# Edge tables of a graph-network kernel loaded for four turns at once, with a table of their own for the scatter pass

## What is computed

```python
# layer 0, twice; layer 3 the same with 8 heads of 16 features
xj = (x @ Wl + bl)[src]
e = leaky_relu(xj + (x @ Wr + br)[dst], 0.2)
logits = e @ att
ex = exp(logits - segment_max(logits, dst)[dst])
out = segment_sum(ex / segment_sum(ex, dst)[dst] * xj, dst)
# layer 2: the score is a sum of two numbers per edge, its message a gathered row
score = leaky_relu(logit[dst] + logit_src[src] + b1)
# layer 1: the edge's two ends are exchanged: its sums go to the unsorted side
agg = segment_sum(exp(leaky_relu(p1[src] + p2[dst])) * emb[dst], src)
```

## Time and profile before

| | us |
|---|---|
| median of 3 runs | 14,991.36 |
| lowest, highest | 14,955.31, 14,998.18 |
| the profiled execution, its time | 14,998.32 |
| its span, first to last instruction | 14,996.4 |
| POOL busy in the span | 9,489.8 (63%) |
| PE busy | 11,026.0 (74%) |
| DVE busy | 7,973.5 (53%) |
| ACT busy | 5,541.4 (37%) |

### The profile page before, as it was taken

How to read it: one execution, slowest core, us unless ns; L and a number is a source line. 1 busy time by engine, 2 the same in 40 slices (tenths; PEclk the granted TensorE clock), 3 DMA queues, 4 the chain that set the end, 5 groups by cost and what they waited for, 6 DMA issues and landing times.

```text
span 14996.4 us, 278163 instructions
## 1 busy us (share of the span) xinstructions
PE 11026.0 (74%) x60653; PEld 8678.6 (58%) x60653; DVE 7973.5 (53%) x29240; ACT 5541.4 (37%) x14105; POOL 9489.8 (63%) x8593
## 2 busy tenths in 40 slices
PE   5777777777777778888888875555555767777776
PEld 4666666666666666666666653344344556666664
DVE  6555555555555555555555553333333566666666
ACT  1444444344444444333333343333333622222223
POOL 3666666466666657888888865566666255655555
PEclk7887788788778775766666765555555877888777
DMA  3111111221111113444444452222222221222222
GB/s 87 45 45 44 44 45 45 88 80 44 45 44 45 44 40 44 39 39 39 39 39 39 39 104 58 44 45 45 45 45 45 60 52 48 50 49 49 50 50 56
DMA packets 808955, 748.01 MB, mean 50 GB/s; under 512 B 264685, under 2 KB 691174, under 8 KB 808254
## 3 DMA queue, kind: packets, MB, share of 16 engines
q0 software_dynamic: 453440, 550.05, 21.1%
q1 hardware_dynamic: 354814, 191.38, 4.9%
HBM read 548.62 MB, written 192.13 MB: 49 GB/s over the span
## 4 chain that ended last, share of the span: by engine, by line
PE 27%; another core or an unknown queue 15%; issue 13%; DMA 9%; DVE 7%; ACT 6%; POOL 2%; SPq 1%; DVEq 1%; ACTq 0%; POOLq 0%
DMA scatter_s<-dst_side 8%; PE bank L738 8%; PE bank L721 3%; PE bank L722 3%; PE bank L1214 3%; ACT oh_e L826 2%; PE bank L1220 2%; PE bank L1229 2%; PE bank L747 2%; PE bank L705 1%; POOL scatter_s L1181 1%; DVE agg L960 1%; DVE lrelu L915 1%; DVE agg L951 1%
## 5 line engine op out<-in xcount | busy, mean ns | idle before, releaser
L738 PE MATMUL bank<-rows,oh_e 128*128 128x130 f32 x9984 | 2172.6, 376 | 1578.7 <-ACT oh_e L826 1172.1
L1181 POOL DMA_INDIRECT scatter_s<-dst_side x1664 | 2568.6, 1544 | 551.9 <-DMA scatter_s<-dst_side 267.1
L738 PEld LDWEIGHTS bank<-rows,oh_e 128*128 128x128 f32 x9984 | 1804.0, 264 | 1918.7 <-issue 1036.4
L826 ACT ACTIVATE oh_e<-bank,weight,minus_w 128x128 f32<-128x128 f32 x4992 | 1880.3, 459 | 2378.4 <-remote 1620.8
L951 DVE SCALAR_TENSOR_TENSOR agg<-agg,rescale,bank 128x130 f32 x4992 | 1683.4, 337 | 1636.6 <-remote 792.6
L722 PE MATMUL bank<-rows,ident 128*128 128x128 f32 x9984 | 2335.9, 319 | 144.8 <-issue 141.1
L687 POOL DMA_INDIRECT rows<-gather_c,edge_sb x1664 | 1650.9, 992 | 1122.4 <-issue 443.9
L687 POOL DMA_INDIRECT rows<-gather_b,edge_sb x1664 | 1672.5, 1005 | 1061.9 <-issue 423.0
L687 POOL DMA_INDIRECT rows<-gather_a,edge_sb x1664 | 1669.1, 1003 | 1008.5 <-issue 412.0
L687 POOL DMA_INDIRECT rows<-gather_s,edge_sb x1664 | 1574.3, 946 | 1061.2 <-issue 443.2
L722 PEld LDWEIGHTS bank<-rows,ident 128*128 128x128 f32 x9984 | 1894.7, 235 | 159.7 <-issue 157.6
(11 more groups left out here) (352 smaller groups left out, 18169.2 us busy)
## 6 DMA issues: line engine op xcount, KB each, us to landing
rows<-gather_a,edge_sb POOLq DMA_INDIRECT x1664
rows<-gather_b,edge_sb POOLq DMA_INDIRECT x1664
scatter_s<-dst_side POOLq DMA_INDIRECT x1664
rows<-gather_s,edge_sb POOLq DMA_INDIRECT x1664
rows<-gather_c,edge_sb POOLq DMA_INDIRECT x1664
rows<-scatter_s SPq DMA_DIRECT2D x56, 455.0 KB, 6.3
scatter_s<-zeros SPq DMA_DIRECT2D x64, 390.0 KB
edge_sb<-edge_tab SPq DMA_DIRECT2D x520, 40.0 KB
```

The costliest lines, as they stand in the source:

```text
L738: ins = e.matmul(sum_bank(g)[:, (g % 2) * AW:(g % 2) * AW + L.aw], oh_e[:, g % 8, :], r, start=True, stop=True)
L826: e.activation(oh_e[:, g % 8, :], bank[7][:, (g % CH) * P:(g % CH + 1) * P], ACT.Relu, bias=weight[:, it.slot(2, 2), g:g + 1], scale=minus ...
L1181: e.indirect_dma_start(scatter_s[k], bass.IndirectOffsetOnAxis(ap=S_.target[:, it.slot(1), g:g + 1], axis=0), S_.summed[:, g % 8, :], None ...
```

## The change

`edge_tab` keeps only the two parts that the gather passes read, and a row of it holds four groups: 128 numbers (512 bytes) per partition. `edge_sb` has eight places of 32 columns, two sets of four turns. SyncE loads a set at every fourth turn, on semaphores of its own (`edge_tables_in`, two of them), ahead of that turn's other tables; `tables_in_slot` counts one DMA less. GpSimd waits for the set's semaphore at every fourth turn and no longer for `tables_in_slot`. The loops of SyncE and GpSimd have bodies of eight turns.

The scatter pass gets its own table `edge_tab_s` of 48 columns per group. It loads one group per turn as before, into the same memory (`S_.edges`).

In the preparation `edge_tab` is stored in 13 pieces, one per 8 groups, each issued in the next tile's round; `edge_tab_s` is stored in one DMA after all of them and after the last store of `gather_a`. E0's opening no longer waits for it. Only the clearing of `agg` does, since the staging area lies in `agg`; `E0.clearing` says so. `tables_saved` counts the 13 pieces and the two row tables.

```diff
+def quad_of(it):
+    return Turn(it.n // QUAD, it.j, it.per // QUAD)
...
-    ET = 5 * G
-    edge_tab = dram("edge_tab", (NG, P, ET))
+    assert NG % (2 * QUAD) == 0
+    ET, ES = 2 * G, 3 * G
+    edge_tab = dram("edge_tab", (NG // QUAD, P, QUAD * ET))
+    edge_tab_s = dram("edge_tab_s", (NG, P, ES))
...
-        edge_sb = sb("edge_sb", [P, U, ET])
+        edge_sb = sb("edge_sb", [P, 2 * QUAD, ET])
...
+            def edges_of(c):
+                w.wait_ge(edges_made.at(c))
+                lo, hi = c * GC // QUAD, (c + 1) * GC // QUAD
+                e.dma_start(edge_tab[lo:hi, :, :].rearrange("q p k -> p q k"),
+                            edge_stage[:, c * GC:(c + 1) * GC, :].rearrange("p (q g) k -> p q (g k)", g=QUAD)).then_inc(tables_saved, 16)
...
+                if c:
+                    edges_of(c - 1)
                 sp_dense0(e, D, "D", c)
-            w.wait_ge(edges_made.at(SC - 1))
-            e.dma_start(edge_tab.rearrange("g p k -> p g k"), edge_stage).then_inc(edge_saved, 16)
             for t in range(SC, NBT):
                 sp_dense0(e, D, "D", t)
+            e.dma_start(edge_tab_s.rearrange("g p k -> p g k"), edge_stage_s).then_inc(edge_saved, 16)
...
-            es = edge_stage[:, c * GC:(c + 1) * GC, :]
-            part = lambda n: es[:, :, n * G:(n + 1) * G]
+            part = lambda stage, n: stage[:, c * GC:(c + 1) * GC, n * G:(n + 1) * G]
             ps = lambda n: bank[c % 2][:, n * P:(n + 1) * P].rearrange("p (g k) -> p g k", k=G)
             mt = mtmp.rearrange("p (g k) -> p g k", k=G)
             w.wait_ge(tile_turned.at(c))
-            own.did(e.tensor_copy(part(0).bitcast(I32), ps(1)))
-            own.did(e.tensor_copy(part(1), ps(0)))
-            own.did(e.tensor_scalar(part(2), ps(0), 0.0, NEG, ALU.is_lt, ALU.mult))
+            own.did(e.tensor_copy(part(edge_stage, 0).bitcast(I32), ps(1)))
+            own.did(e.tensor_scalar(part(edge_stage, 1), ps(0), 0.0, NEG, ALU.is_lt, ALU.mult))
             own.did(e.tensor_scalar(mt, ps(0), P - 0.5, NEG, ALU.is_gt, ALU.mult))
-            own.did(e.tensor_copy(part(3), ps(1)))
-            own.did(e.tensor_copy(part(4), ps(2)))
-            w.wait_ge(own.so_far())
-            e.tensor_tensor(part(2), part(2), mt, ALU.add).then_inc(edges_made.sem, 1)
+            own.did(e.tensor_copy(part(edge_stage_s, 1), ps(1)))
+            own.did(e.tensor_copy(part(edge_stage_s, 2), ps(2)))
+            w.wait_ge(own.so_far())
+            own.did(e.tensor_tensor(part(edge_stage_s, 0), part(edge_stage, 1), mt, ALU.add))
+            w.wait_ge(own.so_far())
+            e.tensor_copy(part(edge_stage, 1), part(edge_stage_s, 0)).then_inc(edges_made.sem, 1)
...
-                self.tab = counts.landing("tables_in_slot", U, 3 + heads, NG)
+                self.tab = counts.landing("tables_in_slot", U, 2 + heads, NG)
+                self.edges_in = counts.landing("edge_tables_in", 2, 1, NG // QUAD)
...
-                e.dma_start(edge_sb[:, u, :], edge_tab[bass.ds(i, 1), :, :].rearrange("o p k -> (o p) k")).then_inc(L.tab.sem(it), 16)
+                if it.n % QUAD == 0:
+                    q, k = quad_of(it), it.slot(0, 2 * QUAD)
+                    w.hold_ge(L.edges_in.at(q, lag=2))
+                    e.dma_start(edge_sb[:, k:k + QUAD, :].rearrange("p t k -> p (t k)"),
+                                edge_tab[bass.ds(q.number(), 1), :, :].rearrange("o p k -> (o p) k")).then_inc(L.edges_in.sem(q), 16)
                 e.dma_start(oh_rows[0:3, u, :], onehot_tab[:, bass.ds(i * (G * P), G * P)]).then_inc(L.tab.sem(it), 16)
...
-            turns(e, NG, 0, turn)
+            long_turns(e, NG, 0, turn, 2 * QUAD)
...
-                u = it.slot()
-                w.hold_ge(L.tab.at(it))
+                u, k = it.slot(), it.slot(0, 2 * QUAD)
+                if it.n % QUAD == 0:
+                    w.hold_ge(L.edges_in.at(quad_of(it)))
...
-                                             bass.IndirectOffsetOnAxis(ap=edge_sb[:, u, g:g + 1].bitcast(I32), axis=0)
+                                             bass.IndirectOffsetOnAxis(ap=edge_sb[:, k, g:g + 1].bitcast(I32), axis=0)
...
+            for point in L.clearing:
+                w.wait_ge(point)
             e.memset(agg[:, :, :], 0.0).then_inc(L.cleared.sem, 1)
...
-                                    view(edge_sb[:, u, 2 * G:], [(0, heads), (1, G)]), ALU.add).then_inc(L.masked.sem, 1)
+                                    view(edge_sb[:, it.slot(0, 2 * QUAD), G:], [(0, heads), (1, G)]), ALU.add).then_inc(L.masked.sem, 1)
...
+        E0.clearing = [(edge_saved, 16)]
```

More of the change, by code:

```diff
@@ L22 @@
 LEAD = 10
+QUAD = 4
 AW = 136
@@ L317, in build @@
         row_made = counts.events("group_rows_made", 1, 1)
-        row_saved = counts.sem("group_rows_saved")
+        tables_saved = counts.sem("group_tables_saved")
         ones_in_rows = counts.sem("ones_in_onehot_rows")
@@ L329, in build @@
         kcol = big2[:, 2 * S:2 * S + SC * P]
-        edge_stage = big1[:, 0:NG * ET].rearrange("p (g k) -> p g k", k=ET)
-        spare = lambda lo, n: big1[:, NG * ET + lo:NG * ET + lo + n]
+        edge_stage_s = big1[:, 0:NG * ES].rearrange("p (g k) -> p g k", k=ES)
+        spare = lambda lo, n: big1[:, NG * ES + lo:NG * ES + lo + n]
         mtmp = spare(0, P)
@@ L336, in build @@
         row8 = spare(3 * P, R8)[0:NG, :]
+        edge_stage = spare(4 * P + R8, NG * ET).rearrange("p (g k) -> p g k", k=ET)
         def tile_set(k):
@@ L371, in sp_prep @@
                     w.wait_ge(row_made.at(0))
-                    e.dma_start(row_tab1, row1).then_inc(row_saved, 16)
-                    e.dma_start(row_tab8, row8).then_inc(row_saved, 16)
+                    e.dma_start(row_tab1, row1).then_inc(tables_saved, 16)
+                    e.dma_start(row_tab8, row8).then_inc(tables_saved, 16)
                 if c == COLS_AT + 1:
@@ L393, in sp_prep @@
                 w.wait_ge(source_saved.at(c))
-            e.wait_ge(edge_saved, 16)
-            e.wait_ge(row_saved, 16 * 2)
+            e.wait_ge(tables_saved, 16 * (2 + SC))
             e.wait_ge(ones_in_rows, 1)
@@ L639, in __init__ @@
                 self.masked = one("masked")
-                self.zeroing, self.zeroed = [], None
+                self.zeroing, self.zeroed, self.clearing = [], None, []
             def w_last(self, it, lag, c):
@@ L1114, in __init__ @@
                 self.free, self.saved, self.n = free, saved, 0
+                self.edges = flat3(edge_sb)[:, 0:U * ES].rearrange("p (u k) -> p u k", k=ES)
                 self.src_rows = self.part(U * G * P // 2).bitcast(BF16).rearrange("p (u n) -> p u n", u=U)
@@ L1290, in turn @@
                             e.tensor_scalar(S_.same[:, g % 8, :], bank[2][:, (g % CH) * P:(g % CH + 1) * P],
-                                            edge_sb[:, v, 3 * G + g:3 * G + g + 1], weight[:, it.slot(1, 2), g:g + 1],
+                                            S_.edges[:, v, G + g:G + g + 1], weight[:, it.slot(1, 2), g:g + 1],
                                             ALU.is_equal, ALU.mult).then_inc(S_.same_made.sem, 1)
@@ L1318, in turn @@
                     w.wait_ge(S_.leaky.at(it))
-                    e.tensor_tensor(logit[:, 0:G], logit[:, 0:G], edge_sb[:, u, 2 * G:3 * G], ALU.add).then_inc(S_.masked.sem, 1)
+                    e.tensor_tensor(logit[:, 0:G], logit[:, 0:G], S_.edges[:, u, 0:G], ALU.add).then_inc(S_.masked.sem, 1)
                     w.wait_ge(S_.count.at(it, G - 1))
@@ L1322, in turn @@
                     w.wait_ge(S_.aim.at(it, lag=1))
-                    e.tensor_scalar(S_.target_f, edge_sb[:, u, 3 * G:4 * G], dump_row[:, 0:1], -1.0, ALU.subtract, ALU.mult
+                    e.tensor_scalar(S_.target_f, S_.edges[:, u, G:2 * G], dump_row[:, 0:1], -1.0, ALU.subtract, ALU.mult
                                     ).then_inc(S_.less.sem, 1)
@@ L1328, in turn @@
                     w.wait_ge(S_.moved.at(it))
-                    e.tensor_tensor(S_.target_f, S_.target_f, edge_sb[:, u, 3 * G:4 * G], ALU.add).then_inc(S_.aim_f.sem, 1)
+                    e.tensor_tensor(S_.target_f, S_.target_f, S_.edges[:, u, G:2 * G], ALU.add).then_inc(S_.aim_f.sem, 1)
                     w.wait_ge(S_.aim_f.at(it))
```

9 lines of the change are left out of this document (5 added, 4 removed).

## The result

The changed kernel takes 15,008.9 us (median of 20 runs), the kernel before 14,976.0 (20 runs). The ratio is 1.0023, with a 95% interval of 1.0016 to 1.0030: 34 us slower by the ratio (the medians differ by 33), where 48 us faster was forecast. That is inside the 0.3% that I had called the same, but the interval leaves no doubt of the direction, and it is the other one.

What follows compares the result with a forecast made beforehand. No engine was full; GpSimd's gather turns, waiting mostly for TensorE's side sums, were taken to set the pace. Terms -44 - 5 + 1 = -48 us gave 14,945 us, range 14,820 to 15,050.

Steps and rivals of the forecast that it cites:

- Longer bodies: SyncE's and GpSimd's loops of eight turns instead of four: between 0 and -0.5 us a turn, taken as 0.
- GpSimd's wait: Gather passes: GpSimd waits for one load every fourth turn, so TensorE's waits for rows go: -44 us, bounds 0 and 149.
- SyncE's instructions: Gather loops: fewer edge loads for SyncE to issue with register addresses: -5 us, from a possible 0 to 41 us.
- the transfers: Gather passes: 104 edge loads of 40 KB become 26 of 64 KB, hidden as transfers, costed at 0.
- Start of E0: End of preparation: edge table stored in pieces, another table last, shifting first gathers and clearing: -3 to +6 us, taken +1.
- E2 out of step: Rival, chance 0.14: unequal load groups and GpSimd starting without waits keep E2's turns slow, +119 us: 15,110 or 15,065.
- SyncE's slow groups: Rival, chance 0.17: slow load issue is the loops' price, so edge loads count far more: 14,778 or 14,853 us.
- each removed load on the path: Rival, chance 0.01: issue and landing of all 312 removed gather-pass loads are saved, 718 us: 14,280 us.
- Nothing moves: Rival, chance 0.20: GpSimd starts turns earlier, then waits for the side sums; TensorE's row waits become others: 14,990 us.

Runs made afterwards that it cites:

- e1: Kernel before with only GpSimd's loop bodies of eight turns instead of four: ratio 1.0041 to the kernel before.
- g2: The kernel of e4 with SyncE's and GpSimd's loop bodies of eight turns: ratio 0.9987 to the kernel before.
- g4: The kernel of e4 repeated on another chip: ratio 0.9951 to the kernel before.
- h1: The changed kernel repeated, on the same chip as h2: median 14,912.8 us, ratio 1.0008 to the kernel before.
- h2: The changed kernel with a hint naming the closing branch of GpSimd's loop: median 14,856.0 us, ratio 0.9967 to the kernel before.
- e2: Kernel before with only SyncE's loop bodies of eight turns instead of four: ratio 1.0003 to the kernel before.
- e4: Kernel before, 104 edge loads per pass kept but on two semaphores of their own, GpSimd waiting for these alone: ratio 0.9963 to the kernel before.
- h3: The kernel before, unchanged, on the chip of h1 and h2: one profiled execution, 95-turn loops E0 to E3 of 2378, 2375, 2406, 2491 us.
- g1: The changed kernel with the closing-branch hint on GpSimd's loop, on the chip of g4: ratio 0.9953 to the kernel before.
- e3: The changed kernel with edge tables for two turns instead of four, loop bodies of four and an extra SyncE mask wait: ratio 0.9978 to the kernel before.
- g3: The kernel of e4 with the closing-branch hint on DVE's loops: ratio 0.9949 to the kernel before.
- f1: The kernel before, unchanged, on the chip with the short times: ratio 1.0003 to the kernel before.
- f2: The changed kernel, unchanged, on the chip with the short times: ratio 1.0018 to the kernel before.

## Why the prediction was wrong

**The step that failed** is *Longer bodies*: "No row shows what a loop's end costs [...] I take 0." The cost is 61 us (e1), 54 (g2 against g4, SyncE's longer bodies with it) and 57 (h1 against h2), all on GpSimd, since SyncE's longer bodies alone cost nothing (e2). My bound, 0 to -0.5 us a turn, had only gains in it: I took a loop's end to be a fixed price that fewer ends would lower. It is a price that depends on whether the body is still held when the branch is taken, and doubling the body went past that. And the trace of before did show that such a price exists. In the scatter pass DVE's loop body of four turns has 567 instructions, and at each of its ends DVE's timeline has a gap of some 3 us with no releaser:

```profile
6070.20 1.37 DVE L1290 TENSOR_SCALAR dst_side<-bank,edge_sb,weight 128x128 f32<-128x128 f32 x4 [2.71 <-issue]
```

Counting instructions per body would not have settled the term, but it would have forbidden the 0: 231 instructions cost 0.25 us at a loop's end, 567 cost 2.8 us, and GpSimd was about to have 453, in between. At 11 taken branches in each of four passes the loss could be 2.3 x 44 = 101 us. The second interruption in E3 adds 1.6 to 1.8 us at 11 loop ends, some 19 us, which no row of before could show. About 57 us in all reach the end, since GpSimd has some slack in a turn: in the first turns of h2's iterations it waits 2.1 to 3.2 us ahead of the third gather (medians of E0, E1 and E3), in those of h1 0.1 to 0.2.

**GpSimd's wait, -44 us.** The mechanism was right, and the term too small by a little: e4, which has it alone, gives 55 and 73 us. The measure that I took it from was not a good one, and its nearness is partly luck. On one chip, TensorE's waits for rows in E3, E0 and E1 are 32.5 us in the kernel before (h3) and 24.9 in e4: 8 us less, where 55 are gained. The lines of E3, h3 and then e4:

```profile
PE bank L721 <- DMA rows<-gather_c,edge_sb: 9.0, 9, 1.9
```

```profile
PE bank L723 <- DMA rows<-gather_c,edge_sb: 0.7, 1, 0.7
```

GpSimd's own idle time at the starts of E3's turns, 61 us and 7, is nearer to the gain. Most of the gain is thus in waits under other names; which ones was not traced. E3's turn fell from 26.22 us (h3) to 25.78 (e4) and 25.74 (h2), by half as much again as forecast (26.6 to 26.3).

**SyncE's instructions, -5 us, and the transfers, 0.** Not to be told from zero: the hinted changed kernel with 26 edge loads a pass (g1, 0.9953) and e4's with 104 (g4, 0.9951) agree within their intervals on one chip; on the other it is 0.9967 (h2) and 0.9963 (e4). Loading for four turns at once bought nothing that these runs can tell from zero; giving the edges a semaphore of their own bought the whole gain. The longer bodies came with the former. (The 2.0 us that the prediction sets against the landing for one rival are given in the Trainium skill for DMAs that GpSimd issues; the table loads are SyncE's.)

**Start of E0, +1 us.** The gathers came 0.6 us later and the clearing 1.4. Right, and small.

**The rivals.** The one that ends slower, E2 out of step, named the pass that lost most (its turn 25.64 us, 2436.06/95, against 25.17 before) but not the cause. GpSimd starts turns without waiting for the tables in e4, and the groups are unequal in g1; E2 takes 2,383 (g4) and 2,393 us there. In h1 to h2 16 us of E2's loss are the loop ends. h2 is still 19 us above h3, e3 32 above e4, g1 10 above g4: unequal groups may cost E2 10 to 30 us. But e2, without either, was long as well, and these are single executions, so that part stays open. The totals leave room for it: e3, with unequal groups and short bodies, is 0.0015 (22 us) above e4, with intervals that overlap. *SyncE's slow groups* and *each removed load on the path* are excluded by the equality of g1 and g4. *Nothing moves* is excluded by e4.

**The sum with the failed term mended**: the gain of e4 and the loss of e1, both on the chip of h, give 0.9963 + 0.0041 = 1.0004, where h1 measured 1.0008. The first comparison had 1.0023 and g2 (the same loops without the tables for four turns) 0.9987. Part of these 54 us may be E3's second interruption, which g2 has in E2 instead and shorter, and part the chip, which moves a near cancellation of two effects of 60 us; the runs don't separate them. The fastest versions are g3, g4 and g1, 0.9949 to 0.9953: DVE's hints add nothing to g4.

## What to carry to other kernels

Before you lengthen or unroll a hardware loop, count the instructions between its branches on each engine and look in the trace for loops of such a length or longer: the idle time at their ends, with no releaser, is the price, and it counts on the engine that has least slack at that point. If your length lies between one that is free and one that is not, put the price in the range. Look a few instructions past the branch as well: there can be a second interruption, which depends on where the loop lies in the program. When an edit needs a side effect (here bodies of eight for tables of four turns), cost the side effect as a change of its own; the gain may be to be had without it. Where a wait covers more than the waiting engine reads, try splitting the semaphore before reducing the transfers: here the first gave 55 to 73 us and the second nothing measurable.

## What the runs showed of the hardware that I had not expected

The hint for the closing branch cuts the time from branch to next instruction from 2.6 to 0.22-0.41 us on GpSimd and from 2.8 to 0.53 us on DVE. Without it, one loop end can hold a second interruption of some 1.1 to 1.9 us, six register instructions behind the branch: in E3 of the changed kernel (all three profiled executions) and in E2 of g2, at every one of the 11 loop ends, and nowhere else.

The same kernel takes 14,900 to 15,000 us on two chips and 12,872 us on a third. The granted clock is part of it (0.94 against 0.81 in E0), but not all: E2 runs at 0.50 on all of them, and its turn takes 25.2 us in the trace of before (2390.75/95) and 20.0 in f1. What differs in the traces is how long engines wait for semaphore updates beside which the profile finds no sender that had just ended ("remote"). The costliest group of ScalarE, first in the trace of before and then in f1 (count, busy us, mean ns, idle us and what ended most of it):

```profile
L826 ACT ACTIVATE oh_e<-bank,weight,minus_w 128x128 f32<-128x128 f32 x4992 | 1880.3, 459 | 2378.4 <-remote 1620.8
```

```profile
L826 ACT ACTIVATE oh_e<-bank,weight,minus_w 128x128 f32<-128x128 f32 x4992 | 1876.2, 456 | 1482.2 <-PE bank L747 1409.6
```

In f1 no wait at all is put down to a remote release; in the trace of before they are 6,880 us on ScalarE, DVE and GpSimd together. The reason is not known from these runs. On that chip GpSimd is the bound, and the changed kernel is slower by another route. The first row is E0 in f1, the second in f2:

```profile
383.02:2321.25 1938.23, 1475.01 (x1520) 0.94 0.22 55
```

```profile
383.44:2342.55 1959.11, 1495.77 (x1520) 0.94 0.21 54
```

E0 is 20.9 us longer, and GpSimd's 1,520 gathers are busy 20.8 us longer. Neither the hint nor the loop's start changes that, and why the same gathers take longer was not found.
